# Branch two's row maxima over blocks of 32 queries of all heads, with the causal mask inside the contraction

## The reference, cut to what matters

```python
scores = jnp.einsum('bhqd,bhkd->bhqk', q, k) / SCALE                 # branch one
scores = jnp.where(causal_mask, -1e12, scores)
attn = jnp.einsum('bhqk,bhkd->bhqd', jax.nn.softmax(scores, axis=-1), v)
...
att = jnp.einsum('bhqd,bhkd->bhqk', q, k) / jnp.sqrt(jnp.float32(D)) # branch two
att = jnp.where(mask, att, -jnp.inf)
y = jnp.einsum('bhqk,bhkd->bhqd', jax.nn.softmax(att, axis=-1), v)
```

## Time and profile before

| | before |
|---|---|
| median of 3 runs | 1533.01 us |
| profiled execution: its own time / its span | 1532.75 us / 1530.9 us |
| PE (matmul) busy | 1434.0 us, 94% |
| PEld (weight load) busy | 1105.5 us, 72% |
| DVE busy | 1154.5 us, 75% |
| ACT busy | 1002.3 us, 65% |
| POOL busy | 555.6 us, 36% |
| mean granted TensorE clock | 0.977 |

### The profile page before, as it was taken

One profiled execution on the slowest core, in us unless ns is written; L12 is line 12 of the kernel. 1 busy time (PEld: TensorE's weight loads), 2 busy tenths in 40 slices (PEclk: granted clock), 3 DMA queues, 4 the chain that ended last, 5 costly groups with the idle time before them and its releaser, 6 DMA issues.

```text
span 1530.9 us, 36632 instructions
## 1 busy us (share of the span) xinstructions
PE 1434.0 (94%) x14742; PEld 1105.5 (72%) x14742; DVE 1154.5 (75%) x2351; ACT 1002.3 (65%) x1585; POOL 555.6 (36%) x551
## 2 busy tenths in 40 slices
PE   4689999999999999999999999999999999999985
PEld 3557777777777777777777777777777777777753
DVE  6667786887878687887868778786878878687613
ACT  2147766676677667676767667676766767676772
POOL 5233333443343344334333433433344343433012
PEclk9589999999999999999999999999999999999998
DMA  6556766546655654665666456656546566675200
GB/s 146 90 105 120 114 106 115 108 98 88 115 113 113 109 107 94 91 112 115 111 110 114 94 91 103 122 103 112 115 96 105 87 124 108 104 115 97 29 2 14
DMA packets 202617, 153.71 MB, mean 100 GB/s; under 512 B 32416, under 2 KB 197920, under 8 KB 202384
## 3 DMA queue, kind: packets, MB, share of 16 engines
q1 hardware_dynamic: 184016, 149.78, 54.7%
q10 hardware_dynamic: 18432, 1.58, 0.9%
HBM read 82.62 MB, written 67.11 MB: 98 GB/s over the span
## 4 chain that ended last, share of the span: by engine, by line
PE 69%; DVE 21%; ACT 4%; issue 4%; POOL 1%; DMA 0%; DVEq 0%; POOLq 0%; ACTq 0%
PE psm L211 21%; PE ps L211 21%; PE pse L211 12%; PE psv L211 9%; DVE R L691 8%; DVE rt L753 2%; PE ps L297 2%; DVE th L803 1%; DVE ks L680 1%; ACT pB L1033 1%; ACT PT L1047 1%; DVE ks L682 1%; PE ps L363 1%; ACT pse L1051 1%; DVE xs L623 1%
## 5 line engine op out<-in xcount | busy, mean ns | idle before, releaser
L691 DVE TRANSPOSE_TENSOR_REDUCE R<-psm 128x32 f32<-128x1024 f32 x384 | 478.4, 1246 | 170.2 <-PE psm L211 169.5
L1047 ACT ACTIVATE PT<-pse 128x1024 f32<-128x1024 f32 x384 | 392.5, 1022 | 242.9 <-PE pse L211 242.9
L1051 ACT ACTIVATE pse<-maskb 128x512 f32<-128x512 bf16 x510 | 285.4, 592 | 8.1
L211 PE MATMUL psm<-qsB,ks 96*128 96x512 f32 x768 | 226.4, 417 | 29.7 <-DVE R L691 29.6
L211 PE MATMUL pse<-qsB,ks 98*128 98x512 f32 x768 | 216.3, 403 | 6.9 <-issue 3.5
L1239 POOL TENSOR_TENSOR ts_<-ts_,pA 128x512 f32<-128x512 f32 x32 | 37.3, 1165 | 448.1 <-DVE pA L629 448.1
L211 PEld LDWEIGHTS psm<-qsB,ks 96*128 96x128 f32 x768 | 132.9, 191 | 68.7 <-DVE R L691 43.5
L211 PEld LDWEIGHTS pse<-qsB,ks 98*128 98x128 f32 x768 | 141.6, 189 | 43.3 <-issue 6.0
L1247 POOL TENSOR_TENSOR tc_<-tc_,ts_ 128x512 f32<-128x512 f32 x64 | 82.1, 1282 | 227.6 <-DVE ts_ L649 227.5
L211 PE MATMUL psm<-maskb,identb 128*128 128x512 bf16 x512 | 156.4, 387 | 0.0
L211 PE MATMUL pse<-qsA,ksA 98*128 98x128 bf16 x1536 | 127.8, 220 | 9.1 <-ACT pse L1051 7.6
(11 more groups left out here) (186 smaller groups left out, 2520.2 us busy)
## 6 DMA issues: line engine op xcount, KB each, us to landing
scrB<-pB SPq DMA_DIRECT2D x32, 1536.0 KB, 5.9
qsB<-scrB SPq DMA_DIRECT2D x384, 128.0 KB, 6.1
scrA<-pA SPq DMA_DIRECT2D x32, 384.0 KB, 2.6
qsA<-scrA SPq DMA_DIRECT2D x192, 64.0 KB
ksA<-scrA SPq DMA_DIRECT2D x192, 64.0 KB
xs<-in_x SPq DMA_DIRECT2D x16, 256.0 KB, 8.3
out<-zz SPq DMA_DIRECT2D x16, 256.0 KB, 3.6
qsA<-cA ACTq DMA_DIRECT2D x64, 8.0 KB, 2.5
```

The lines of the kernel that those rows point to most:

```text
L211: return e.matmul(o, l, r, start=start, stop=stop, skip_group_check=True)
L691: e.tensor_reduce(red, MX[:].rearrange("p i (c q) -> p (i c) q", q=32), AX.X, ALU.max, apply_transpose=True).then_inc(s_mr, 1)
L1047: e.activation(PT[g % 4], EX[:], ACT.Exp, scale=(8.0 ** -0.5, 0.125)[br]).then_inc(s_pt, 1)
L1051: e.activation(EX[:, i].rearrange("p (h q) -> p h q", h=4), bc(maskb[:], 4), ACT.Copy).then_inc(s_sd, 1)
```

## The change

Branch two's maxima are computed over other blocks. A unit is now 128 keys by 64 queries of all 16 heads: two banks of 32 queries x 16 heads (`WIDE`). The four blocks of 32 queries in a diagonal tile of 128 keys each have their own mask; it is added by 32 more rows of the contraction. Rows 96 to 127 of the new stationary tile `ksm` hold, for each of the four blocks, -2^99 where a key lies behind the query of that row, and rows 96 to 127 of `qsB` hold a unit matrix of 32 queries, repeated (`same`). There are no mask matmuls in these slots any more. Off the diagonal `ks1` is used as before. Since `ksm` depends on the batch and on the tile of keys, GpSimd copies `ks1` into it twice per batch (`prep_km`, in its slots 4 and 8). Rows 96 and 97 of `qsB` are overwritten by the maxima's row in each batch, so SP writes `same` into them again ahead of each half of the reads (one more small DMA per half; the counts on `d_br` go from 96 to 112), and the rows 98 to 127 once in the start. `prep_ks` moves from slot 4 to slot 2 on VectorE, and the DMAs of the maxima's row from slot 4 to slot 2 on ScalarE's queue.

```diff
+WIDE = [(0, 0), (0, 2), (0, 4), (0, 6), (1, 4), (1, 6)]
...
+            def wide_scores(b, u, i):
+
+                s, (kt, q0) = b % 2, WIDE[u]
+                keys, queries = slice(128 * kt, 128 * kt + 128), slice(32 * (q0 + i), 32 * (q0 + i) + 32)
+                o = MX[:, i].rearrange("p (h q) -> p h q", h=H)
+                if kt == q0 // 4:
+                    mm(o, ksm[:, (q0 + i) % 4], qsB[s][:, :, queries], True, False)
+                else:
+                    mm(o, ks1[s][0:96, keys], qsB[s][0:96, :, queries], True, False)
+                return mm(o, ks2[s][0:96, keys], qsB[s][0:96, :, queries], False, True)
...
-                    w.wait_ge(d_br[b % 2][u // 3], 96 * (b // 2 + 1))
+                    for hh in range(2):
+                        w.wait_ge(d_br[b % 2][hh], 112 * (b // 2 + 1))
+                    w.wait_ge(d_mk, 64)
                     w.wait_ge(s_ks, b + 1)
-                for i in range(2):
-                    t = scores(br, b, MX, u, i, 96, True)
-                if UNITS[u][0] == UNITS[u][1]:
+                    if u not in (2, 3):
+                        w.wait_ge(s_km, 2 * b + 1 + u // 4)
+                if br == 1:
                     for i in range(2):
-                        t = mask(MX, i, False)
+                        t = wide_scores(b, u, i)
+                else:
+                    for i in range(2):
+                        t = scores(br, b, MX, u, i, 96, True)
+                    if UNITS[u][0] == UNITS[u][1]:
+                        for i in range(2):
+                            t = mask(MX, i, False)
...
+            def setup_masks():
+                w.wait_ge(d_mk, 32)
+                e.tensor_copy(ksm[96:128], zz[0][96:128])
+                e.tensor_copy(same[:], zz[1][0:32, 0:2, :].rearrange("p i c -> p (i c)")).then_inc(s_mk, 1)
...
-                    if k == 4 and body:
+                    if k == 2 and body:
                         max_row(1, c)
...
+            def prep_km(b, kt):
+                w.wait_ge(s_ks, b + 1)
+                if kt or b:
+                    w.wait_ge(s_mx, unit(1, b, 1) + 1 if kt else unit(1, b - 1, 5) + 1)
+                e.tensor_copy(ksm[0:96], bc(ks1[b % 2][0:96, 128 * kt:128 * kt + 128], 4)).then_inc(s_km, 1)
...
+                    if k in (4, 8) and n1 < NB:
+                        prep_km(n1, k // 8)
...
+                e.dma_start(qsB[s][96:98, 8 * hh:8 * hh + 8, :].bitcast(F32), bc(same[0:2].bitcast(F32), 8)).then_inc(d_br[s][hh], 16)
...
+            for s in range(2):
+                e.dma_start(qsB[s][98:128].bitcast(F32), bc(same[2:32].bitcast(F32), H)).then_inc(d_mk, 16)
```

More of the change, by code:

```diff
@@ L60, in build @@
         ksA = [sb(f"ksA{i}", [98, H, S], BF16) for i in range(2)]
-        qsB = [sb(f"qsB{i}", [98, H, S], F32R) for i in range(2)]
+        qsB = [sb(f"qsB{i}", [128, H, S], F32R) for i in range(2)]
         ks1 = [sb(f"ks1{i}", [98, S], F32R) for i in range(2)]
+        ksm = sb("ksm", [128, 4, 128], F32R)
+        same = sb("same", [32, S], F32R)
         ks2 = [sb(f"ks2{i}", [98, S], F32R) for i in range(2)]
@@ L135, in build @@
         d_br = [[sem(f"d_br{i}{j}") for j in range(2)] for i in range(2)]
+        d_mk = sem("d_mk")
         d_c = [sem(f"d_c{i}") for i in range(2)]
@@ L148, in build @@
         s_pa0, s_ra, s_pa1, s_pa2 = (sem(n) for n in ("s_pa0", "s_ra", "s_pa1", "s_pa2"))
-        s_pb0, s_tr, s_pb1, s_pb2, s_kt, s_ks = (sem(n) for n in ("s_pb0", "s_tr", "s_pb1", "s_pb2", "s_kt", "s_ks"))
+        s_pb0, s_tr, s_pb1, s_pb2, s_kt, s_ks, s_km, s_mk = (sem(n) for n in ("s_pb0", "s_tr", "s_pb1", "s_pb2", "s_kt", "s_ks", "s_km", "s_mk"))
         s_y, s_z, s_sq, s_ms, s_x2, s_xl = (sem(n) for n in ("s_y", "s_z", "s_sq", "s_ms", "s_x2", "s_xl"))
@@ L685, in max_unit @@
                 g = unit(br, b, u)
-                kt, qt, h0 = UNITS[u]
-                red = R0[br][:, h0:h0 + 8, 4 * qt:4 * qt + 4] if kt == 0 else R1[br][:, h0:h0 + 8, :]
+                if br == 0:
+                    kt, qt, h0 = UNITS[u]
+                    red = R0[0][:, h0:h0 + 8, 4 * qt:4 * qt + 4] if kt == 0 else R1[0][:, h0:h0 + 8, :]
+                else:
+                    kt, q0 = WIDE[u]
+                    red = (R1 if kt else R0)[1][:, :, q0 - 4 * kt:q0 - 4 * kt + 2].rearrange("p h q -> p q h")
                 w.wait_ge(s_mx, g + 1)
@@ L897, in _ @@
             setup_values()
+            setup_masks()
             prep_blo(0)
@@ L966, in _ @@
                             prep_xlo(n2)
-                    if k == 2 and odd and moe:
-                        moe_hg(p, 4)
+                    if k == 2:
+                        if n1 < NB:
+                            prep_ks(n1)
+                        if odd and moe:
+                            moe_hg(p, 4)
                     if k == 3:
@@ L976, in _ @@
                             prep_blo(n2)
-                        if n1 < NB:
-                            prep_ks(n1)
                     if k == 5:
@@ L1287, in _ @@
             for c in range(-1, NB + 3):
-                n2, p = c + 2, c // 2 - 1
+                n1, n2, p = c + 1, c + 2, c // 2 - 1
                 even, odd = c % 2 == 0, c % 2 == 1
@@ L1354, in stack_b @@
                     for hh in range(2):
-                        w.wait_ge(d_br[s][hh], 96 * (b // 2))
+                        w.wait_ge(d_br[s][hh], 112 * (b // 2))
                 e.dma_start(scrB[s].rearrange("x p t -> p x t"), pB[:].bitcast(F32).rearrange("p u k a t -> p (u k a) t")).then_inc(d_bw[s], 16)
@@ L1385, in _ @@
                     load_x(1)
+                if i == 3:
+                    e.dma_start(zz[0][96:128], I["above"]).then_inc(d_mk, 16)
+                    e.dma_start(zz[1][0:32, 0:2, :].rearrange("p i c -> p (i c)"), I["same"]).then_inc(d_mk, 16)
                 for dst, src in pairs:
@@ L1388, in _ @@
             stack_a(0)
+            w.wait_ge(s_mk, 1)
+            for s in range(2):
+                e.dma_start(qsB[s][98:128].bitcast(F32), bc(same[2:32].bitcast(F32), H)).then_inc(d_mk, 16)
             stack_b(0)
@@ L1439, in layout @@
     a["mask"] = np.where(np.arange(128)[:, None] > np.arange(128)[None, :], np.float32(BIG), np.float32(0))
+    r, k, j = np.arange(32)[:, None, None], np.arange(128)[None, None, :], np.arange(4)[None, :, None]
+    a["above"] = np.where(k > 32 * j + r, np.float32(-2.0 ** 99), np.float32(0))
+    a["same"] = (np.arange(32)[:, None] == np.arange(256)[None, :] % 32).astype(np.float32)
     a["pri"] = (8 - np.arange(8, dtype=np.float32)).reshape(1, 8)
```

## The result

| | before | after |
|---|---|---|
| median | 1533.05 us (1531.5 to 1533.37, 4 runs) | 1474.55 us (1472.63 to 1475.46, 4 runs) |
| ratio to before | 1 | 0.9619 [0.9602, 0.9635] |
| profiled execution: its own time / its span | 1532.75 / 1530.9 us | 1472.63 / 1470.8 us |
| mean granted TensorE clock | 0.977 | 0.978 |

The change saves 58.5 us; forecast was 1475 us, 58 less than before. (The median of before, 1533.01 in front, is 1533.05 with the run taken beside after's.)

The account below looks back on a forecast made before the run. TensorE, busy 1264.08 of 1295 us, was taken as the bound. Gains of 54.6, 12.4 and 3.5 less 6.9, 1.7, 3 and 1 gave 57.9 us off 1532.75: forecast 1475 us, range 1464 to 1496.

Parts of the forecast that it names:

- The masks: TensorE, slots 6, 8, 9, 11: removing a mask matmul pair saves 0.44 us each, 54.6 us in all.
- clips: Even slot 6 and odd slot 9: ScalarE's mask seeds limit TensorE's gain, giving back 6.9 and 1.7 us.
- only 0.43 of the 0.86 us that TensorE wins there: Even slot 6: exp scores wait for ScalarE's seeds, so part of the 0.42 + 0.44 gain is lost, -6.9 us.
- prep_ks (12.4): VectorE, slot 4 to 2: slot 5's reduction comes in time, ending TensorE's waits of 0.42 (even) and 0.38 us (odd).
- the row (3.5): Maxima's row DMAs issued in slot 2: the "issue" waits before slot 6's exp scores go, 3.5 us.
- Short runs: TensorE's wide score matmuls: moving operand in 16 runs of 32 instead of 4 of 128 costs 0, at most 9 us.
- Rival C: TensorE reads short runs markedly slower; 0.078 us more per matmul cancels everything; 0.04, with anything else costing more than the masks.
- GpSimd's copies: Two copies into ksm per batch, 0.7 us each, hold VectorE 0.1 us per round: -3 us, bounds 0 and -34.
- Rival B: GpSimd's copies hold VectorE between slots 3 and 5, decided from about 0.8 us: 1484, bound 1506; chance 0.12, alone or with A.
- Rival A: VectorE takes over: late reductions lose half the masks' gain in slots 6 and 8, 14 us, giving 1489; chance 0.16.
- Rival D: Better than the sum: no clip, no hold, the start gives something; up to 70.5 us, 1462; chance 0.07.
- The hole in slot 2: VectorE idle 1.06 (even) and 1.18 us (odd) there, covering prep_ks; without it slot 3's reduction comes up to 1 us later.

Follow-up runs that it names:

- a_masks: The changed kernel with the pair of mask matmuls put back ahead of the wide scores in the four diagonal slots: 1510.28 us.
- b_ks2_row2: The kernel before with only prep_ks and the DMAs of the maxima's row moved to slot 2, masks and units as before: 1508.24 us.
- a_row4: The changed kernel with the DMAs of branch two's maxima's row back in slot 4: 1482.89 us.
- a_km_twice: The changed kernel with each of GpSimd's two copies into ksm per batch made twice: 1501.76 us.
- a_ks4: The changed kernel with prep_ks back in slot 4 on VectorE, the row's DMAs staying in slot 2: 1532.04 us.
- a_ks4_kmlate: The changed kernel with prep_ks back in slot 4 and GpSimd's first copy into ksm moved behind prep_r1: 1492.26 us.

## Why the prediction was right, and where its parts were not

The sum was 57.9 us and 58.5 were measured. The places were right; the shares of the three edits were not, and that the sum hits to 0.6 us is luck. The masks with all that belongs to the wide form stood in it at 54.6 - 8.6 - 3 - 1 = 42.0 us and brought 33.7; the two moves stood at 15.9 and brought 24.8. The two misses, 8.3 too much and 8.9 too little, cancel. I give the mean distance, over rounds 1 to 29, from the first maxima matmul of a slot to that of the next (us, odd round / even round), worked out from the traces; a wait ahead of slot 6's maxima thus counts in slot 5:

| slot | before | both moves | after |
|---|---|---|---|
| 5 | 3.52 / 3.38 | 2.88 / 2.75 | 2.87 / 2.76 |
| 6 | 5.18 / 4.91 | 4.73 / 4.80 | 4.57 / 4.80 |
| 8 | 3.73 / 3.21 | 3.74 / 3.21 | 3.41 / 2.78 |
| 9 | 4.03 / 4.62 | 4.03 / 4.61 | 3.82 / 4.27 |
| 11 | 4.58 / 3.81 | 4.58 / 3.81 | 4.18 / 3.38 |

- **The masks (54.6, less clips of 8.6): over-sized.** Last on top of the two moves the wide units bring 1508.24 - 1474.55 = 33.7 us, and the masks alone cost 35.7 (a_masks). The pair's 0.44 us is won whole in the even slot 8 and nearly so in slot 11, by three quarters in the odd slot 8 (0.33) and the even slot 9 (0.34), by half in the odd slot 9 (0.21), by a third in the odd slot 6 (0.16), and not at all in the even slot 6. There the chain from slot 5's exp scores over exp and seeds to slot 6's exp scores sets the time: 709.23 - 706.57 = 2.66 us in b_ks2_row2 and 692.60 - 689.94 = 2.66 in after. The step that failed is "only 0.43 of the 0.86 us that TensorE wins there": as a limit it was right, since `prep_ks` alone brought 0.40 us (3.28 to 2.88) and reached it, but then it belongs wholly to the mask; the 0.22 us on top came from the row's move. The odd slot 6 has a limit that I did not see, and it is the seeds too: slot 6's exp scores start 0.75 us after the seeds do (692.60 - 691.85) in the even rounds of b_ks2_row2 and after, and in the odd rounds of after; only in the odd rounds of b_ks2_row2 are there 0.91 us, and the difference is the 0.16 won. What holds the odd slot 8 and the even slot 9 below 0.44 stays open, and so does half of the loss in the odd slot 9.
- **prep_ks (12.4) and the row (3.5): under-sized.** Together 24.8 us. I took the idle time of a row as the price of the wait; it was 0.42 of 0.73 us up to the last of the maxima. I gave the row's move only the waits for the transfer, and missed what its DMA issues cost on ScalarE's own queue: 0.22 us in each even round. And the two edits are no sum: 11.9 and 0 alone, 24.8 together, since with one made TensorE runs into what the other removes. "With the gains above, this wait would have grown" was right: 8.3 us in a_row4, from a wait with a long tail and from those issues.
- **Short runs (0, at most 9):** 0.24 against 0.2325 us is 744 x 0.0075 = 5.6 us by the rows, within the bounds (the rows more in the contraction are 32, not the twelve of the prediction; neither adds a column); form, copies and start together cost 2.0 us (a_masks against b_ks2_row2), within what the intervals allow. Rival C's size is a tenth of what it needed (0.078). By the Trainium skill (SBUF — State Buffer, "Door 1: The DMA port swizzle") it should be 0; the rows show a little more.
- **GpSimd's copies (-3; 0.7 us each):** 0.61 us, and a cast was held in one round only. Rival B's point of decision, 0.8 us, stands: 0.61 + 0.21 = 0.82 us, and a second copy past it costs 27 us. The Trainium skill (GPSIMD Engine Reference, "Key points") says that GpSimd and VectorE contend on SBUF interfaces that they share, if the VectorE operation runs in a 2-port mode or has two SBUF inputs; the contention is there in a_km_twice, with 1.45 us for a cast of 0.41. The cast has one input, and in which mode it ran no trace shows.
- **Rival A** (VectorE takes over) did not come: 20 waits for the reduction against 47. **Rival D** had the masks' full value; the clips stood against it.
- **The hole in slot 2** was cover, as said. What I had not priced is the other use of the move: with the copy on GpSimd waiting for `prep_ks`, the early place is what the new form rests on (57.5 us in a_ks4).
- Of the signs, the mask count, the seeds' wait and the end of the "issue" waits came true. "Waits for the reduction in the even slot 10 alone" was nearly so: 20 are left, 14 of them there, 0.44 us in the round shown.

## What to carry to other kernels

Price a wait by the distance from one start to the next with and without it, not by the idle time in its row: for pipelined matmuls that idle time was 0.42 us of 0.73. When a DMA issue is moved, count also what it costs on the engine whose queue it leaves: here 0.22 us a round, in rounds that never waited for the transfer. Ask of each gain which chain takes over within the same slot, and give a limit shared by two edits to neither alone; only an experiment with one of them tells whose it is. When an edit gives an in-order engine an operation with a new wait, look first at what is queued behind it: the same copy cost nothing, or 40 us, by its place among its neighbours. And look at the granted clock before a whole difference is called waiting: some 11 of those 40 us were TensorE's clock, which fell after the waits.

## What the runs showed of the hardware

- VectorE's cast stays held through GpSimd operations that follow one another without a gap: 1.45 us over two of them (0.41 alone), in all 28 rounds of a_km_twice up to 1320 us. The other way round too: L1300 on GpSimd takes 0.95 us where it starts 0.06 us after the cast (686.52 against 686.46), and 0.73 in a_km_twice (L1301 there), where it was the cast that was held.
- In the even slot 6 the four matmuls of 512 columns took 1.05 us behind a wait and 0.91 without it; the first of them took the difference. Slots 8 and 10 have the same longer first matmul without a wait, so its cause is open.
- After waits of TensorE of up to 1.9 us (a_ks4) the granted clock fell from 1.00 to 0.50, and exp scores of 1.17 us took 1.99; it came in 7 of 14 odd rounds. In a_ks4_kmlate, with no wait over 0.8 us, it did not come.
- Two DMA issues on ScalarE's queue in slot 4 put ScalarE's next exp 0.22 us later (1.10 us against 0.88 after its scores' start).
- A copy of 96x512 on GpSimd, `ks1` to `ksm`, takes 0.61 us.
- A moving operand in 16 runs of 32 elements costs 0.24 us per 512 columns, in 4 runs of 128 it is 0.2325.
